# A mixture-of-experts stage whose slot table is built by one-hot matmuls and whose blocks gather and scatter their own rows

## What is computed

```python
H, I, E_ROUTED, TOP_K = (256, 704, 7, 2)
def _expert(h, g, u, d):
    return einsum('...i,hi->...h', silu(h @ g.T) * (h @ u.T), d)
out = _expert(x, sg, su, sd)                       # shared expert, all tokens
probs = softmax(x @ wr.T + rb, axis=-1)
scores, idx = top_k(probs, TOP_K)
scores = scores / scores.sum(axis=-1, keepdims=True)
w = sum(scores[..., None] * one_hot(idx, E_ROUTED), axis=-2)
for e in range(E_ROUTED):
    out = out + w[..., e:e + 1] * _expert(x, rg[e], ru[e], rd[e])
```

## Time and profile before

| | |
|---|---|
| median of three executions | 2150.76 us |
| the profiled execution, device time | 2150.42 us |
| its span, first to last instruction | 2148.5 us |
| granted TensorE clock, mean | 0.952 |
| PE, DVE, ACT, POOL busy | 90%, 71%, 54%, 27% |
| q0, DMAs that POOL issues | 3072 packets, 8.39 MB |
| q8, instructions | 134 packets, 2.20 MB |

### The profile page before, as it was taken

One profiled execution on the slowest core, in us unless ns is written; L12 is line 12 of the kernel. 1 busy time (PEld: TensorE's weight loads), 2 busy tenths in 40 slices (PEclk: granted clock), 3 DMA queues, 4 the chain that ended last, 5 costly groups with the idle time before them and its releaser, 6 DMA issues. The chain is left out here.

```text
span 2148.5 us, 47582 instructions
## 1 busy us (share of the span) xinstructions
PE 1939.7 (90%) x18832; PEld 1807.5 (84%) x18832; DVE 1524.4 (71%) x2830; ACT 1153.8 (54%) x1928; POOL 575.9 (27%) x543
## 2 busy tenths in 40 slices
PE   4699999999999999999999999996593499999988
PEld 2599999999999999999999999994373399999987
DVE  3577777777777777777777777774776167777745
ACT  3155656556555666565655655564752045555532
POOL 1223222332233222232233223301111603333342
PEclk8799999999999999999999999998696699999998
DMA  3666666666666666566666666652414445555522
GB/s 130 168 167 171 150 156 164 160 163 156 161 156 169 156 153 173 152 164 157 161 165 160 154 159 165 164 127 62 152 46 153 147 146 205 195 184 190 200 69 79
DMA packets 165281, 328.03 MB, mean 153 GB/s; under 512 B 58544, under 2 KB 96944, under 8 KB 161632
## 3 DMA queue, kind: packets, MB, share of 16 engines
q1 hardware_dynamic: 162016, 316.96, 53.4%
q0 software_dynamic: 3072, 8.39, 1.2%
HBM read 138.70 MB, written 28.44 MB: 78 GB/s over the span
## 5 line engine op out<-in xcount | busy, mean ns | idle before, releaser
L380 ACT COPY a_pT<-a_pst 128x512 f32<-128x512 f32 x768 | 421.6, 583 | 439.5 <-PE a_pst L598 439.3
L386 ACT ACTIVATE a_probs<-a_probs,a_nmax 128x1601 f32<-128x1601 f32 x256 | 418.9, 1636 | 146.2 <-DVE a_probs L424 146.2
L598 PE MATMUL a_pst<-a_id,a_probs 128*128 128x128 f32 (+1 forms) x3328 | 452.1, 274 | 28.8 <-ACT a_pT L380 26.2
L424 DVE TENSOR_SCALAR_CACHE_REDUCE a_probs<-a_pss 128x1608 f32<-128x1608 f32 x256 | 467.3, 1825 | 14.5 <-PE a_pss L587 12.4
L598 PEld LDWEIGHTS a_pst<-a_id,a_probs 128*128 128x128 f32 (+1 forms) x3328 | 381.6, 140 | 72.1 <-ACT a_probs L386 36.2
L348 POOL TENSOR_TENSOR a_tick<-a_tick 128x1 f32<-128x1 f32 x62 | 12.2, 197 | 979.1 <-DMA a_raw<-in_ctxT 964.1
L442 DVE TENSOR_SCALAR a_khi<-a_psk,a_bk 128x402 fp32r<-128x402 f32 x250 | 158.6, 634 | 144.7 <-PE a_psk L552 140.2
L353 POOL TENSOR_TENSOR a_clo<-a_raw,a_chi 128x402 fp32r<-128x402 f32 x240 | 246.6, 1060 | 4.8
L587 PE MATMUL a_pss<-a_kst,a_bd 96*128 96x402 f32 x1024 | 240.5, 357 | 6.8 <-DVE a_klo L444 6.8
L550 PE MATMUL a_pso<-a_whi,a_chi 128*128 128x256 f32 x806 | 241.3, 299 | 0.4 <-issue 0.4
L552 PE MATMUL a_pso<-a_whi,a_clo 128*128 128x256 f32 x806 | 227.0, 282 | 0.0
(11 more groups left out here) (225 smaller groups left out, 3572.0 us busy)
## 6 DMA issues: line engine op xcount, KB each, us to landing
a_kst<-a_khi SPq DMA_DIRECT2D x1024, 100.5 KB, 2.5
a_kst<-a_klo SPq DMA_DIRECT2D x512, 100.5 KB, 2.6
a_raw<-in_ctxT SPq DMA_DIRECT2D x60, 804.0 KB, 5.6
e_gur<-in_wgu SPq DMA_DIRECT2D x24, 1408.0 KB, 6.2
e_dr<-in_wd SPq DMA_DIRECT2D x24, 768.0 KB, 4.9
e_xb<-rows_scr SPq DMA_DIRECT2D x30, 256.0 KB
a_bd<-q_scr SPq DMA_DIRECT2D x192, 32.0 KB, 2.0
rows_scr<-f_zero SPq DMA_DIRECT2D x4, 1408.0 KB, 12.3
```

Of the source, the lines that this page charges most:

```text
L380: nc.scalar.copy(pT[:, p % HALF, 4 * i:4 * i + 4, :], ps_t[:, i % 2, :].rearrange("p (t q) -> p t q", q=P)).then_inc(t_copied_act, 1)
L386: nc.scalar.activation(pr, pr, ACT.Exp, bias=nmax[:, b, p:p + 1], scale=-1.0, accum_out=esum[:, b, p:p + 1]).then_inc(probs_ready, 1)
L424: nc.vector.tensor_scalar(probs[:, p % 2, :].rearrange("p (b k) -> p b k", b=QK), ps_s[:, :, 0:KQ], -1.0, None, ALU.mult, ALU.min, accum_o ...
L598: mm = nc.tensor.transpose(ps_t[0:r, i % 2, (t % 4) * P:(t % 4 + 1) * P], probs[:, p % 2, t * P:t * P + r], id_sb[:])
```

## The change

1. `circuit_ffn` ends with the bias addition into a tile `logits` that stays in SBUF. It no longer fills the routed rows with zeros (one zero tile is stored instead), and it stores the normed rows twice, behind that zero tile, so that each of the 4096 (choice, token) pairs has its own row. The tables aren't stored.
2. `experts` does the softmax and chooses by maximum, twice, with ties to the lower index. Its PE turns the first rows ahead of that and counts ranks with 17 accumulated matmuls, which give the prefix sums over tiles as well. DVE plans with a scan, and forms each row's slot as high and low digits.
3. One-hots of the digits (`high` by 44, `low` by 128) for the 32 (choice, tile) pairs are made on DVE inside block 0, the products on POOL and ACT; 32 matmuls after block 1 (`fill_table`) give, for each of the 44 x 128 slots, the row that sits there; `read_table` in block 2 turns it into indices `x_at` and `y_at`.
4. POOL gathers each routed block's rows straight into `xb` and scatters its result straight to the pair's own row in `ys_scr` (padding goes to spare rows), two indirect DMAs of 128 rows each. The 64 long-burst DMAs, SP's row loads of routed blocks and its result stores go. After the last, SP fetches the results with eight plain loads.
5. The gated product h is written to the PSUM bank that its chunk came from (`hidden`), so both of its splits read PSUM, and PE waits for the split of chunk i - 4 to refill the bank. The down product waits for the split chunk by chunk. POOL's low part of d is cut in three instructions.
6. All loops are unrolled.

```diff
@@ circuit_ffn
-            for g in range(NG):
-                r0 = HEAD * BR + ZROWS * g
-                sp.dma_start(rows_scr[r0:r0 + ZROWS, :].rearrange("(j p) d -> p j d", p=P),
-                             zero[:].unsqueeze(1).to_broadcast([P, ZROWS // P, D])).then_inc(stored, 16)
+            sp.dma_start(rows_scr[0:P, :], zero[:]).then_inc(stored, 16)
...
+                for k in range(TOPK):
+                    r0 = (1 + k * NT + t0) * P
+                    sp.dma_start(rows_scr[r0:r0 + n * P, :].rearrange("(t p) d -> p t d", p=P), a[:, tiles(g), :]).then_inc(stored, 16)
...
+            nc.vector.tensor_tensor(lg[:], ps_l[:, 0:NT * E].rearrange("p (t e) -> p t e", e=E), rb_sb[:].unsqueeze(1).to_broadcast([P, NT, E]),
+                                    ALU.add).then_inc(l_copied, 1)
@@ experts, sync
+            load_gu(0, 1)
+            load_rows(0, 0)
+            for dst, src in ((cnt_sb, counts), (tri_sb, tri), (id_sb, ident)):
                 sp.dma_start(dst[:], src).then_inc(plan_loaded, 16)
...
+                    if b == LAST + 1:
+
+                        for z in range(2):
+                            sp.wait_ge(y_stored[z], 16 * BJ * (NBLK // 2))
+                        for q in range(NG):
+                            for k in range(TOPK):
+                                r0 = (1 + k * NT + GT * q) * P
+                                sp.dma_start(fetched[:, GT * q:GT * (q + 1), k, :], ys_scr[r0:r0 + GT * P, :].rearrange("(t p) d -> p t d", p=P)).then_inc(fetched_loaded[q], 16)
@@ experts, gpsimd
+            def gather_rows(b):
+
+                pool.wait_ge(x_filled, b - 1)
+                for j in range(BJ):
+                    i = BJ * (b - HEAD) + j
+                    nc.gpsimd.indirect_dma_start(xb[:, b % 2, j, :], None, rows_scr, bass.IndirectOffsetOnAxis(x_at[:, i:i + 1], 0)).then_inc(rows_gathered[b % 2], 16)
+
+            def scatter_rows(b):
+
+                pool.wait_ge(y_copied, b - HEAD + 1)
+                for j in range(BJ):
+                    i = BJ * (b - HEAD) + j
+                    nc.gpsimd.indirect_dma_start(ys_scr, bass.IndirectOffsetOnAxis(y_at[:, i:i + 1], 0), yb[:, b % 2, j, :], None).then_inc(y_stored[b % 2], 16)
...
+            pool.wait_ge(high_hot, 1)
+            nc.gpsimd.tensor_tensor(out=values[:, :, 0:SLOTS], in0=values[:, :, SLOTS:].bitcast(F32),
+                                    in1=iota[:, 1:1 + KT2].unsqueeze(2).to_broadcast([P, KT2, SLOTS]), op=ALU.mult).then_inc(high_values, 1)
             split_d(1, 0, 1)
...
+            pool.wait_ge(table_ready, 1)
+            gather_rows(HEAD)
+            gather_rows(HEAD + 1)
+            for b in range(HEAD + 1, LAST + 2):
+                w = b - HEAD + 1
+                split_d(w, b % 2, w // 2 + 1 if w % 2 == 0 else (w + 1) // 2)
+                if b - 2 >= HEAD:
+                    scatter_rows(b - 2)
+                if b + 1 <= LAST:
+                    gather_rows(b + 1)
+            scatter_rows(LAST)
@@ experts, vector
+                bank = ps_gu[:, (EC * s + c) % 4, :]
+                up = bank[:, BR:2 * BR] if c < EC - 1 else bank[REST:2 * REST, 0:BR]
+                nc.vector.tensor_tensor(hidden(s, c), up, silu[0:P if c < EC - 1 else REST, c % 2, :], ALU.mult).then_inc(h_done, 1)
...
+            def low_ones(z):
+
+                c = slice(z * KT2 // 4, (z + 1) * KT2 // 4)
+                if z == 0:
+                    ch.wait()
+                nc.vector.tensor_tensor(low_hot[:, c, :], iota.unsqueeze(1).to_broadcast([P, KT2 // 4, P]),
+                                        low[:].rearrange("p k t -> p (k t)")[:, c].unsqueeze(2).to_broadcast([P, KT2 // 4, P]), ALU.is_equal).then_inc(low_hot_ready, 1)
...
+            route()
             split_rows(0, 0)
             for z in range(2):
                 split_gu(0, 1, z)
+            plan()
             gate(0, 0, 0)
@@ experts, tensor
-                if not (isinstance(i, int) and i < 4):
-
-                    pe.wait_ge(h_done, i - 3)
+                if not (i < 4):
+
+                    pe.wait_ge(h_split, i - 3)
...
+            def fill_table():
+
+                pe.wait_ge(low_hot_ready, 4)
+                pe.wait_ge(value_ready, 1)
+                for c in range(KT2):
+                    mm = nc.tensor.matmul(ps_x[:, 1, 0:2 * SLOTS], low_hot[:, c, :], values[:, c, :], start=(c == 0), stop=(c == KT2 - 1))
+                mm.then_inc(table_filled, 1)
...
+            for d in range(NT + 1):
+                mm = nc.tensor.matmul(ps_y[:, 0, 0:(NT + 1) * E], (one_sb if d else tri_sb)[:], taken[:, NT - d:2 * NT - d + 1, :].rearrange("p t e -> p (t e)"),
+                                      start=(d == 0), stop=(d == NT))
+            mm.then_inc(ranks_filled, 1)
             start_block(0, 0)
-            for it in range(3):
+            for it in range(NALL // 2):
                 body(it)
-            with nc.Fori(3, NALL // 2 - 2, engines=(pe.engine,), hint_back_edge=True) as it:
-                body(it)
```

More of the change, by code:

```diff
@@ L1056, in _, with experts @@
                     mm.then_inc(l_filled, 1)
-def experts(nc, x2_scr, rows_scr, top_scr, wgt_scr, ys_scr, wgu, wd, ident, tri, blocks, out):
+def experts(nc, x2_scr, rows_scr, lg, ys_scr, wgu, wd, ident, tri, counts, out):
     with ExitStack() as ctx:
@@ L1093, in experts @@
         ps_gu, ps_y, ps_x = ps("e_psg", [P, 4, 512]), ps("e_psy", [P, 2, 512]), ps("e_psx", [P, 2, 512])
[L1094 to L1097, removed]
+        plan_loaded, acc_loaded = sem("e_ld"), sem("e_al")
@@ L1366, in body @@
                                                 acc[:, BJ * n:BJ * (n + 1), :].rearrange("p j d -> p (j d)"), ALU.add).then_inc(y_added, 1)
-            body(0)
-            body(1)
-            with nc.Fori(2, NALL // 2 - 3, engines=(dve.engine,), hint_back_edge=True) as it:
+            for it in range(NALL // 2):
                 body(it)
-            body(NALL // 2 - 3)
-            body(NALL // 2 - 2)
-            body(NALL // 2 - 1)
         @block.scalar
@@ L1402, in split_h @@
                 act.wait_ge(h_done, i + 1)
-                if c == 0 and not (isinstance(b, int) and b < 2):
+                if c == 0 and not (b < 2):
                     act.wait_ge(y_filled, b - 1)
                 r = slice(0, P if c < EC - 1 else REST)
-                nc.scalar.copy(h_hi[r, s, c, :], h[r, (EC * s + c) % 4, :]).then_inc(h_hi_done, 1)
+                nc.scalar.copy(h_hi[r, s, c, :], hidden(s, c)).then_inc(h_hi_done, 1)
+            act.wait_ge(exp_in, 1)
+            nc.scalar.activation(pr[:], pr[:], ACT.Exp).then_inc(exp_done, 1)
             split_rows(0, 0)
@@ L1556, in build @@
                         ins["rows"], ins["ident"], x1_scr, x1_mv)
-        circuit_ffn(nc, x1_scr, x1_mv, ins["rows"], ins["w1"], ins["b1"], ins["w2"], ins["wr"], ins["rb"], ins["ident"],
-                    x2_scr, rows_scr, top_scr, wgt_scr)
-    experts(nc, x2_scr, rows_scr, top_scr, wgt_scr, ys_scr, ins["wgu"], ins["wd"], ins["ident"],
-            ins["tri"], ins["blocks"], out)
+        with nc.sbuf_tensor("logits", [P, NT, E], F32) as lg:
+            circuit_ffn(nc, x1_scr, x1_mv, ins["rows"], ins["w1"], ins["b1"], ins["w2"], ins["wr"], ins["rb"], ins["ident"],
+                        x2_scr, rows_scr, lg)
+            experts(nc, x2_scr, rows_scr, lg, ys_scr, ins["wgu"], ins["wd"], ins["ident"], ins["tri"], ins["counts"], out)
 def kernel(**inputs):
```

323 lines of the change are left out of this document (153 added, 170 removed).

## The result

The changed kernel takes 2079.21 us (median; 2071.9 to 2082.68) where the kernel before takes 2150.79 beside it: a ratio of 0.9663 (0.9635 to 0.9690). The forecast was 2083. The profiled execution of after has a span of 2080.9 us and a device time of 2082.68; the forecast for the span was 2080.5.

The account below looks back on a forecast made before the run. TensorE (PE), busy for 90% of the span, was taken as the bound. Terms -42.6 + 5.0 - 10.7 - 19.7 = -68.0 us took the span from 2148.5 to 2080.5, 2083 on the median's scale; range 2066 to 2118.

Parts of the forecast that it names:

- Start: Logits to end of block 0: routing moved into the experts, no scatter burst, block 0 done at 1675; -42.6 us (-33 to -51).
- the choice: Maximum-based expert choice on DVE before block 0: 12 tiny operations of 0.28 to 0.3 us, 3.5 us together.
- Slot table: After block 1 and in block 2: 32 matmuls of 3.7 us plus 1.3 us of wait; +5.0 us (3 to 10).
- Routed blocks: Blocks 4 to 25: h in PSUM avoids the shared port, pitch 13.65 instead of 14.14 us; -10.7 us (0 to -12).
- Gathers and scatters: POOL's indirect DMAs inside the blocks: issued by 10.6 us, assumed 3 us landing, three microseconds of cover; cost nothing.
- Unrolled loops: Straight-line expert code: instruction fetching alone should cost nothing; 0, bounds 0 and +10 us.
- Tail: End of block 25 to the end: eight plain loads replace 32 gathers, no starvation; 59.4 against 79.1, -19.7 us (-14 to -21).
- A: Rival, all blocks: short bursts also starve engines, about 0.4 us per indirect DMA, 35 us, giving 2118; chance 0.14.
- D: Rival, all blocks: slower, every indirect DMA beside non-loop code costs 1.1 us, 97 us for 88, giving 2180; chance 0.06.
- B: Rival, routed blocks: POOL becomes the bound, gathers land 0.9 us late, 20 us over 22 blocks, giving 2103; chance 0.07.
- C: Rival, routed blocks: h in PSUM gives nothing, PE waits in bank recycling instead, +10.7 us, giving 2094; chance 0.06.
- E: Rival: better than the sum, block 0 at its lower bound and a gain of 12 in the blocks, 2066 to 2073; chance 0.07.

Follow-up runs that it names:

- v3: Changed kernel with small tables and rows loaded ahead of the weights and POOL's first split of d behind its product for the table: 2072.18 us.
- v2: Changed kernel with small tables and rows loaded ahead of the weights and POOL's first split of d waiting until experts are chosen: 2074.24 us.
- a3_burst16: Changed kernel with 16 spare indirect gathers into unused memory in one burst from block 27 on: 2079.97 and 2079.66 us in the two such runs.
- b2: Kernel before with only the gated product h in PSUM and PE waiting for its split: 2086.11 us, ratio 0.9953.
- a2: Changed kernel with the down product waiting for five split chunks before its first matmul, instead of chunk by chunk: 2091.9 us.

## Why the prediction was right, and where it wasn't

**Start, -42.6 forecast, -39.7 measured.** The mechanism held: no table through DRAM, no scatters ahead of block 0. Taken from the logits, the next stage's first DMA came as forecast, 0.55 us behind them for 0.69, the tables 0.4 us late, the ranks 0.7 and the plan 0.9 us early, and from the plan to the end of block 0 it was 16.3 us for 16.2. The step that failed is the choice: 3.5 us forecast, 7.6 measured, and the first gate matmul came 22.1 us behind the logits for 18.6. DVE's timeline, and POOL's under it:

```profile
1645.08 0.28 DVE L1274 TENSOR_TENSOR e_hit<-e_hit,e_cnt 128x112 f32<-128x112 f32 x1
...
1646.61 1.55 DVE L1273 TENSOR_TENSOR e_hit<-e_pr,e_best 128x112 f32<-128x112 f32 x1
...
1648.20 1.31 DVE L1274 TENSOR_TENSOR e_hit<-e_hit,e_cnt 128x112 f32<-128x112 f32 x1
1649.55 0.27 DVE L1275 TENSOR_REDUCE e_ty<-e_hit 128x16 f32<-128x112 f32 x1
```
```profile
1646.58 1.46 POOL L1179 CAST e_dh<-e_dr 128x1536 fp32r<-128x1536 f32 x1
1648.12 3.77 POOL L1182 TENSOR_TENSOR e_dl<-e_dr,e_dh 128x512 fp32r<-128x512 f32 x3
```

The size of an operation was right (0.28 us), but four of them met POOL's split of d, and their two inputs are in SBUF: 1.55, 1.31, 0.91 and 1.22 us. The reduction between them, with one input, passed in 0.27. I had used just this fact for the routed blocks, and had not asked which POOL work stands beside the moved choice. v3 shows the price with the split away, twelve operations in 3.65 us:

```profile
1634.50 0.27 DVE L1271 TENSOR_REDUCE e_best<-e_pr 128x16 f32<-128x112 f32 x1 [0.65 <-DMA e_id<-in_ident]
...
1637.88 0.27 DVE L1291 TENSOR_TENSOR e_tk<-e_top 128x112 f32<-128x112 f32 x1
```

**Slot table, +5.0 and +5.2.** Right in sum, by errors that cancel. The matmuls took 3.77 us for 3.7. Behind them PE's timeline of block 2:

```profile
1693.76 3.77 PE L1570 MATMUL e_psx<-e_big 128*128 128x88 f32 x32
...
1700.83 0.41 PE L1491 MATMUL e_psg<-e_xh,e_gul 128*128 128x256 f32 x1
...
1702.53 0.63 PE L1506 MATMUL e_psx<-e_id,e_xb 128*128 128x128 f32 x4 [0.56 <-issue]
```

The wait ahead of the transposes is 0.6 us and not 1.3, because PE came later: from 1697.7 to 1701 its matmuls took the 1.2 GHz level (0.41 us a record and 0.21 from one start to the next, for 0.28 and 0.12), after 3.8 us of narrow matmuls. That costs some 1.5 us, for which the sum had no term; against it stand the 0.7 us less of that wait and 0.6 us that the three blocks gain by the waits by chunk. The fall isn't a fixed price of those matmuls: both runs with spare gathers and v2 have the same 32 matmuls in the same 3.77 us with no fall behind them, PE waits 1.1 us ahead of the transposes there, and the block takes 18.3 instead of 19.3 to 19.5 us, so that the table costs 4.2 and not 5.2. The 1.4 us behind the 32 matmuls (windows as in the earlier trace rows) in after, then in a3_burst16:

```profile
1697.36:1698.76 1.40, 1.40 (x10) 1.40 (x10) 0.00 (x0) 0.00 (x0) 0.00 (x0) 0.63 0.00 0
```
```profile
1695.15:1696.55 1.40, 1.40 (x14) 1.40 (x14) 0.00 (x0) 0.00 (x0) 0.00 (x0) 1.00 0.00 0
```

**Routed blocks, -10.7 and -15.9.** The port's part was right (0.42 of a block by b2, 9.3 us for the 22, where 10.7 were forecast). Mis-sized was the pitch that I expected, 13.65 for 13.42: I took the shared blocks of before as the floor, but there too the first matmul of the down product starts 0.27 us behind the last gate matmul instead of 0.12. The waits by chunk, 0.34 us of a block by a2, were part of the change and had no term in the sum. **Gathers and scatters, 0 and 0.** POOL's timeline of a block that begins at 1739.93:

```profile
1741.72 3.80 POOL L1182 TENSOR_TENSOR e_dl<-e_dr,e_dh 128x512 fp32r<-128x512 f32 x3
1745.67 1.02 POOL L1199 DMA_INDIRECT ys_scr<-e_yb,e_yat  x1
...
1748.27 0.98 POOL L1192 DMA_INDIRECT e_xb<-rows_scr,e_xat  x1 [0.30 <-issue]
1749.55 0.96 POOL L1192 DMA_INDIRECT e_xb<-rows_scr,e_xat  x1 [0.30 <-issue]
```

The last is done 10.6 us into the block, as worked out, and PE never waits for it; how long it takes to land, 3 us by assumption, no run shows. **Unrolled loops, 0:** 0.12 us a block in the kernel before; in after it is hidden or within the 13.42.

**Tail, -19.7 and -19.9.** The combines of 3.75, 4.66 and 6.49 us and the last addition fell where they were put. The starvation that made up nearly all of this term was seen only in the first place.

**The rivals.** A and D: the result was measured beside a kernel before that did starve, and there after shows 13.42 in every routed block, as elsewhere; a pair of scatters and a pair of gathers with 9 us between don't starve anyone. A's reading of the row was good (8 gathers did cost 3 to 3.8 us there), its step from 8 in a row to 2 and 2 was not. B: no wait for a gather. C: refuted by b2. E named a gain of 12 in the blocks and had 15.9, but not its start.

That the span came within 0.4 us of the forecast is luck: the blocks gained 5.2 us more than forecast, against a start that gained 2.9 less and logits that came 2.6 later, where nothing was forecast.

What the prediction got right by luck of place is its largest part. 53 of its 62 us from start and tail rest on rows that showed what happened in one place; nothing in them said that it would elsewhere.

## What to carry over

When work is moved, list what each neighbour engine does at its new place, and hold the contention that you know of against every two of them; here one known fact was worth 0.42 us in each block and 4 us, missed, at the start. A pitch seen in the same trace is a floor only if its own gaps have been read. And where a trace shows an engine without instructions, treat what its removal gains as belonging to that trace until a second place shows it: the change was worth 3.4% in one and 0.9% in another.

## What the runs showed of the hardware

- The same 32 indirect scatters, at the same 1.26 us each, starved ScalarE for 20.3 us in one place and not at all on chips 0 and 10. As plain DMAs of the same size they took POOL 17.2 us instead of 41.2.
- A short DVE operation can cost five to seven times its size beside POOL: 0.28 to 1.55 us over 112 elements, 0.17 to 1.22 over 7. A one-hot of 128x1024 took 2.60 us beside POOL's product for the table, 1.21 alone. The other way too: three pieces of the subtraction took 3.80 us in a routed block and 5.61 in block 0, beside two more of these one-hots (1.37 and 1.63 us):

```profile
1671.38 5.61 POOL L1182 TENSOR_TENSOR e_dl<-e_dr,e_dh 128x512 fp32r<-128x512 f32 x3
```

- One wait for five chunks ahead of a product cost 0.28 us at that place in the routed blocks, though the trace names no releaser there; one wait a chunk cost nothing that it shows.
- After the same 32 matmuls of 88 columns (3.77 us) the granted clock fell to the 1.2 GHz level for some 3 us in after and stayed at 2.4 GHz in a3_burst16.
- An indirect DMA of 128 rows of 1 KB cost POOL 0.96 us and a gap of 0.30, as gather and as scatter, in nearly all of its instances.
